# Layer 1 attention in a two-layer kernel: each of a pair's two heads in its own 64 contraction rows

## The reference

```python
xn = _layernorm(x, axis=-1)
x = x + _L1_attn_ref(xn, Wq, Wkv, Wo, bo) + _L1_ffn_ref(xn, inter_w, inter_b, output_w, output_b)
# in _L1_attn_ref: H = 32 heads, G = 8 groups, HD = 16, REP = 4
scores = jnp.einsum('bhqd,bhkd->bhqk', q, k)
scores = jnp.where(causal, -jnp.inf, scores)
weights = jax.nn.softmax(scores * (1.0 / HD ** 0.5), axis=-1)
ctx = jnp.einsum('bhqk,bhkd->bhqd', weights, v)
return jnp.dot(ctx, Wo) + bo
```

## Time and profile before

| | us |
|---|---|
| median of 3 runs | 1771.76 |
| lowest and highest run | 1762.22, 1773.39 |
| span of the profiled execution | 1769.7 |
| granted TensorE clock, mean over the span | 0.980 |

### The profile page before, as it was taken

How to read it: one execution, slowest core, us unless ns; L and a number is a source line. 1 busy time by engine, 2 the same in 40 slices (tenths; PEclk the granted TensorE clock), 3 DMA queues, 4 the chain that set the end, 5 groups by cost and what they waited for, 6 DMA issues and landing times. The chain is left out here.

```text
span 1769.7 us, 27326 instructions
## 1 busy us (share of the span) xinstructions
PE 1668.8 (94%) x8874; PEld 1226.8 (69%) x8874; DVE 1089.3 (62%) x2491; ACT 849.2 (48%) x1595; POOL 708.5 (40%) x735
## 2 busy tenths in 40 slices
PE   6899998999989999999999999789999999999998
PEld 5688887888766666666666666477765555568887
DVE  3556658999747777776777776335657677510222
ACT  3456556443326555555555555344135565653321
POOL 1112213444647566665566665386001111222221
PEclk9999999999999999999999999899979999999999
DMA  7522323220200001000001000364532343131111
GB/s 244 167 73 85 95 84 83 59 66 22 77 13 1 19 19 37 19 19 19 19 19 37 19 19 13 98 203 140 159 48 50 64 81 64 45 98 62 48 48 48
DMA packets 110717, 114.16 MB, mean 65 GB/s; under 512 B 39521, under 2 KB 71745, under 8 KB 110593
## 3 DMA queue, kind: packets, MB, share of 16 engines
q1 hardware_dynamic: 108288, 108.40, 21.8%
q10 hardware_dynamic: 2304, 4.20, 0.6%
HBM read 83.97 MB, written 28.44 MB: 64 GB/s over the span
## 5 line engine op out<-in xcount | busy, mean ns | idle before, releaser
L1490 POOL TENSOR_SCALAR a_p<-a_p,a_rinv 128x640 f32<-128x640 f32 (+7 forms) x256 | 190.6, 748 | 172.6 <-DVE a_rinv L1416 171.6
L1447 ACT ACTIVATE a_p<-a_sm,a_nmax 128x640 f32<-128x640 f32 (+7 forms) x256 | 198.6, 777 | 111.6 <-DVE a_nmax L1408 109.1
L1408 DVE CUSTOM_DVE_ANT_0 a_sm<-ps,maskb 128x640 f32<-128x640 f32 (+7 forms) x256 | 192.5, 752 | 94.7 <-PE ps L1352 91.2
L2334 DVE CUSTOM_DVE_ANT_0 ga_sm<-ps,strip 128x640 f32<-128x640 f32 (+1 forms) x224 | 163.2, 754 | 78.8 <-PE ps L2241 77.3
L2354 ACT ACTIVATE ga_pt<-ps 128x1024 f32<-128x1024 f32 (+1 forms) x192 | 148.1, 810 | 114.8 <-PE ps L2264 114.1
L1364 PE MATMUL ps<-ident,a_p 128*128 128x128 f32 x1152 | 172.1, 274 | 10.6 <-DVE a_pt L1423 10.4
L1364 PEld LDWEIGHTS ps<-ident,a_p 128*128 128x128 f32 x1152 | 132.9, 140 | 33.6 <-issue 10.5
L2394 POOL TENSOR_SCALAR_AFFINE_SELECT ga_pt<-ga_pt 128x512 f32<-128x512 f32 x64 | 40.6, 634 | 286.5 <-ACT ga_pt L2354 286.5
L1379 PE MATMUL ps<-a_pt,vst 128*64 128x512 f32 (+3 forms) x768 | 152.4, 506 | 1.8 <-DVE a_pt L1423 1.1
L1459 ACT COPY a_pt<-ps 128x512 f32<-128x512 f32 x128 | 74.2, 580 | 151.8 <-PE ps L1364 100.0
L1352 PE MATMUL ps<-kh,lq_qh 128*128 128x512 f32 (+3 forms) x384 | 131.7, 397 | 15.4 <-DVE a_nmax L1408 10.6
(11 more groups left out here) (319 smaller groups left out, 3972.1 us busy)
## 6 DMA issues: line engine op xcount, KB each, us to landing
ctx_d<-a_ctxst SPq DMA_DIRECT2D x16, 512.0 KB, 2.9
idx<-ctx_d SPq DMA_DIRECT2D x32, 256.0 KB, 3.8
idx<-wvo_d SPq DMA_DIRECT2D x32, 256.0 KB, 4.5
ga_qst<-qkd SPq DMA_DIRECT2D x42, 128.0 KB, 4.2
f_wr<-in_L_ffn_w SPq DMA_DIRECT2D x18, 256.0 KB, 2.7
x<-in_L_attn_hidden_states SPq DMA_DIRECT2D x16, 256.0 KB, 3.9
op_wo<-in_L_attn_o_w SPq DMA_DIRECT2D x8, 512.0 KB, 4.5
ix_w<-in_L_attn_idx_wq_w SPq DMA_DIRECT2D x64, 64.0 KB, 1.9
```

What stands on the lines that cost most here:

```text
L1408: dve.tensor_tensor_reduce(out=sm[kind][:, 0:w], in0=slots[kind][:, 0:w], in1=maskb[:, MASK_OFF[t]:MASK_OFF[t + 1]], scale=-scale, scalar= ...
L1447: act.activation(p[kind][:, v // 2 % 2, 0:w], sm[kind][:, 0:w], ACT.Exp, bias=nmax[:, v % 4:v % 4 + 1], scale=-1.0, accum_out=rsum[:, v % ...
L1490: pool.tensor_scalar(mine, mine, rinv[:, v % 4:v % 4 + 1], 1.0, ALU.mult, ALU.mult).then_inc(norm_done, 1)
L2334: dve.tensor_tensor_reduce(out=sm[kind][:, 0:w], in0=slots[kind][:, 0:w], in1=strip[:, S - w:], scale=-1.0, scalar=3.0e38, op0=ALU.add, op ...
```

## The change

The two heads of a pair are put 64 rows apart: a = 0 in rows 0 to 47 and a = 1 in rows 64 to 111 (`TILE1` = 64). The keys stand in both places of a single `kst`, without a copy for each a and without zeros. Each score product reads only its head's own rows, 48 of them for `score` and 49 for `keys`, where row 48 (or 112) of `qst` is the head's shift and that of `kst` is 1. Number, width, order, waits and PSUM targets of the matmuls stay, and so do number and size of the transfers. `kst` is prepared by one POOL memset over the whole tile to 1.0, after step 7, in place of POOL's three and DVE's two, and SP waits for that one.

```diff
--- before.py
+++ after.py
@@ -112,7 +112,7 @@
 ATTENTION0 += names("lq_", "raw_in tab_in wh_done wl_done q_mm q_evac add_done qh_done q_lo_done")
 ATTENTION0 += names("oq_", "", raw_in_=4)
 TO_QUERIES = names("oq_", "x_done stat var_done std_done rstd_done xn_done turned xh_done xl_done wh_done wl_done done "
-                   "hi_done lo_done ones_done zero_a zero_b", split_done_=4, cl_done_=4, wvl_done_=4, used_=4, stored=5,
+                   "hi_done lo_done ones_done", split_done_=4, cl_done_=4, wvl_done_=4, used_=4, stored=5,
                    w_in=2)
 LAYER1 = names("", "inv_done norm_done inv_out", raw_out=2, sum_in=2, ctx_in=2, scale_in=2)
 LAYER1 += names("ah_", "high low hidden b1_in", **{"in": 2})
@@ -1690,7 +1690,7 @@
 
 NB1 = 3
 KR1 = 3 * HD1
-KQ1 = 2 * KR1
+TILE1 = 64
 UNITS1 = REP1 * ST
 
 
@@ -1704,7 +1704,7 @@
     b = g % NB1
     sp.wait_ge(first["nt_done"], START + g + 1)
     for h in range(REP1):
-        r0 = KQ1 + h % 2
+        r0 = TILE1 * (h % 2) + KR1
         sp.dma_start(f32(qst[r0:r0 + 1, b, h // 2]).rearrange("o (t n) -> o t n", n=P),
                      nT[h * ST:(h + 1) * ST, g % 2]).then_inc(first["shift_in"][b], 16)
 
@@ -1716,10 +1716,10 @@
     k_v = qkd[:, D:, :].rearrange("l (g p) t -> g l p t", p=HD1)
     for a in range(2):
         for r, l in enumerate((0, 0, 1)):
-            r0 = KR1 * a + r * HD1
-            sp.dma_start(f32(kst[r0:r0 + HD1, b, a, at]), k_v[g][l][:, at]).then_inc(k_in[b], 16)
+            r0 = TILE1 * a + r * HD1
+            sp.dma_start(f32(kst[r0:r0 + HD1, b, at]), k_v[g][l][:, at]).then_inc(k_in[b], 16)
         for r, l in enumerate((0, 1, 0)):
-            r0 = KR1 * a + r * HD1
+            r0 = TILE1 * a + r * HD1
             sp.dma_start(f32(qst[r0:r0 + HD1, b, :, at]), q_v[g][a][l][:, :, at]).then_inc(q_in[b], 16)
 
 
@@ -1783,9 +1783,9 @@
         cr, wr = four(ctxn, 0), four(ctxn, 2)
         slots = [ps[:, 4 + 2 * k:6 + 2 * k, :].rearrange("p b n -> p (b n)") for k in range(2)]
         names = ("x_done", "stat", "var_done", "std_done", "rstd_done", "xn_done", "turned", "xh_done", "xl_done",
-                 "wh_done", "wl_done", "done", "hi_done", "lo_done", "ones_done", "zero_a", "zero_b")
+                 "wh_done", "wl_done", "done", "hi_done", "lo_done", "ones_done")
         (x_done, stat, var_done, std_done, rstd_done, xn_done, turned, xh_done, xl_done, wh_done, wl_done, done,
-         hi_done, lo_done, ones_done, zero_a, zero_b) = (c.sem("oq_" + n) for n in names)
+         hi_done, lo_done, ones_done) = (c.sem("oq_" + n) for n in names)
         split_done, cl_done, wvl_done, used = (
             c.sems(f"oq_{n}_", NS) for n in ("split_done", "cl_done", "wvl_done", "used"))
         stored, w_in = c.sems("oq_stored", NT1), c.sems("oq_w_in", 2)
@@ -1822,8 +1822,7 @@
                         sp.dma_start(qkd[l][m * P:(m + 1) * P, at], f32(o[:, m, at])).then_inc(stored[m], 16)
                     if m == 0:
                         if h == 0:
-                            sp.wait_ge(zero_a, START + 2)
-                            sp.wait_ge(zero_b, START + 3)
+                            sp.wait_ge(ones_done, START + 2)
                         sp.wait_ge(stored[NQ], START + 32 * (h + 1))
                         sp.wait_ge(stored[0], START + 32 * (h + 1))
                         load_group(sp, qkd, qst, kst, q_in, k_in, 0, at)
@@ -1847,12 +1846,7 @@
                     if (half, k) == (0, 5):
                         pool.memset(v32[:, :, :, HD1:], 1.0).then_inc(ones_done, 1)
                     if (half, k) == (0, 7):
-                        pool.memset(f32(kst[:, :, 1]), 0.0).then_inc(zero_b, 1)
-                        pool.wait_ge(zero_b, START + 1)
-                        pool.memset(f32(kst[KQ1:KQ1 + 2, :, 1]), 1.0).then_inc(zero_b, 1)
-                        pool.wait_ge(zero_b, START + 2)
-                        pool.memset(f32(kst[KQ1:KQ1 + 1, :, 1]), 0.0).then_inc(zero_b, 1)
-                        pool.wait_ge(zero_b, START + 3)
+                        pool.memset(f32(kst[:, :, :]), 1.0).then_inc(ones_done, 1)
 
             @block.scalar
             def _(act):
@@ -1956,11 +1950,6 @@
                 for half, k, s, u in steps:
                     dve.wait_ge(split_done[s], START + u + 1)
                     dve.tensor_tensor(cl[:, s], cr[:, s], f32(ch[:, s]), ALU.subtract).then_inc(cl_done[s], 1)
-                    if (half, k) == (0, 6):
-                        dve.memset(f32(kst[:, :, 0]), 0.0).then_inc(zero_a, 1)
-                    if (half, k) == (0, 8):
-                        dve.wait_ge(zero_a, START + 1)
-                        dve.memset(f32(kst[KQ1:KQ1 + 1, :, 0]), 1.0).then_inc(zero_a, 1)
                     if half == 0:
                         continue
                     if k in (2, 3):
@@ -2015,10 +2004,11 @@
                     if v >= 2:
                         pe.wait_ge(first["max_done"], START + v - 1)
                     wide = (t + 1) * P
+                    mine = slice(TILE1 * (h % 2), TILE1 * (h % 2) + KR1)
                     for k0 in range(0, wide, HALF):
                         k1 = min(k0 + HALF, wide)
-                        ins = pe.matmul(slots[v % 2][:, k0:k1], qst[0:KQ1, 0, h // 2, t * P:(t + 1) * P],
-                                        kst[0:KQ1, 0, h % 2, k0:k1], start=True, stop=True)
+                        ins = pe.matmul(slots[v % 2][:, k0:k1], qst[mine, 0, h // 2, t * P:(t + 1) * P],
+                                        kst[mine, 0, k0:k1], start=True, stop=True)
                     ins.then_inc(first["scored"], 1)
 
                 def task(n):
@@ -2149,7 +2139,6 @@
     LAG = 2
     LEAD = 3
     SCALE = HD1 ** -0.5
-    KQ = KQ1
     STEPS = [(0, j) for j in range(4)] + [(1, j) for j in range(8)]
     NSTEP = len(STEPS)
     UNITS = UNITS1
@@ -2236,10 +2225,11 @@
                     if n >= 2:
                         pe.wait_ge(max_done, START + n - 1)
                     w = (t + 1) * P
+                    mine = slice(TILE1 * (h % 2), TILE1 * (h % 2) + KR1)
                     for k0 in range(0, w, HALF):
                         k1 = min(k0 + HALF, w)
-                        ins = pe.matmul(slots[kind][:, k0:k1], qst[0:KQ, b, h // 2, t * P:(t + 1) * P],
-                                        kst[0:KQ, b, h % 2, k0:k1], start=True, stop=True)
+                        ins = pe.matmul(slots[kind][:, k0:k1], qst[mine, b, h // 2, t * P:(t + 1) * P],
+                                        kst[mine, b, k0:k1], start=True, stop=True)
                     ins.then_inc(scored, 1)
 
                 def turn(g):
@@ -2261,8 +2251,9 @@
                     if s == NSTEP - LEAD + 1 and g + 1 < G1 and p == 0:
                         pe.wait_ge(nt_done, START + g + 2)
                     for a in range(2):
-                        ins = pe.matmul(ps[:, 2 * p + a, 0:q1 - q0], kst[0:KQ + 2, b, a, j * P:(j + 1) * P],
-                                        qst[0:KQ + 2, b, p, q0:q1], start=True, stop=True)
+                        mine = slice(TILE1 * a, TILE1 * a + KR1 + 1)
+                        ins = pe.matmul(ps[:, 2 * p + a, 0:q1 - q0], kst[mine, b, j * P:(j + 1) * P],
+                                        qst[mine, b, p, q0:q1], start=True, stop=True)
                     ins.then_inc(st_done[p], 1)
 
                 def weigh(g, s):
@@ -2724,7 +2715,7 @@
                 ci = Ctx(nc, inner)
                 v32 = ci.sb("v32", [P, ST, G1, 2 * HD1])
                 qst = ci.sb("ga_qst", [P, NB1, 2, S], F32R)
-                kst = ci.sb("ga_kst", [P, NB1, 2, S], F32R)
+                kst = ci.sb("ga_kst", [P, NB1, S], F32R)
                 nmax = ci.sb("ga_nmax", [P, 2, UNITS1])
                 nT = idx[0:UNITS1, DT * S:DT * S + 2 * P].rearrange("p (k n) -> p k n", k=2)
                 q_in, k_in = ca.sems("ga_q_in", NB1), ca.sems("ga_k_in", NB1)
```

## The result

| | before | after |
|---|---|---|
| median of four runs, us | 1772.6 | 1838.4 |
| lowest and highest, us | 1762.2, 1773.9 | 1837.6, 1842.4 |
| span of the profiled execution, us | 1769.7 | 1835.9 |
| granted clock, mean over the span | 0.980 | 0.910 |

The ratio is 1.038 (95% interval 1.034 to 1.042): 66 us slower. The forecast was 1802 with a range of 1740 to 1830. Its direction and its cause hold, its size doesn't: twice the loss that was worked out.

What follows compares the result with a forecast made beforehand. PE was taken to have the most work but to be held in a loop with DVE and ACT. Span 1769.7 - 7.5 (memsets) + 3 (projections) + 5 (first group) + 33 (groups 1 to 6) - 1 (last) = 1802 us, range 1740 to 1830.

Steps and rivals of the forecast that it cites:

- The memsets: In outputs_to_queries, one POOL memset for three removes PE's hole and the low clock behind it: -7.5 us (0 to -8).
- Row halves side by side: In attention, a pair's two keys products overlap, up to 4.5 us a group off PE; score gains under 1.
- the prediction's own sign: In the profile after: keys starts of a pair 0.23 us apart, not some ns, would make the overlap step wrong.
- What the overlap is worth: In attention groups 1 to 6, a full-clock group goes from 33.5 to 31 us (bounds 29 and 33.5).
- I count a bit over half: Share of the PE overlap saving in attention expected to come through the loop with DVE: 33.5 to 31 us a group.
- A group at the low clock: An attention group run wholly at clock 0.50 takes 43 us.
- How much of the pace is low: Groups 1 to 6 run two thirds of their pace at 0.50: 39 us each, +33 us over six.
- The projections: Before attention, 24 places where 48-row products stand among 128-row ones cost shape changes: +3 us (0 to twice that).
- First and last group: Attention's first group, mostly low already, +5 us; last group regains the clock, -3 with +2 for shape changes, so -1.
- The clock holds: Rival: only busy time counts, so attention stays at clock 1.00 and gains from overlap: 1746 us, chance 0.23.
- Low clock and no overlap: Rival: attention loses the clock and halves don't overlap, six groups +69 us: about 1845 us, chance 0.07.
- always low: Upper bound of the clock term for groups 1 to 6, at 0.50 throughout: +57 us.

Runs made afterwards that it cites:

- spread_memsets: Kernel before, with POOL's three memsets at steps 7, 12 and 19 of outputs_to_queries instead of all after step 7: 1764.8 us, ratio 0.9971.
- rows64_short: rows64 with DVE's maximum over only the first 256 keys of a row: 1743.1 us, ratio 0.986 to the kernel before.
- rows64: Changed kernel with zero query rows added, so products run over 63 (score) and 64 (keys) rows: 1798.6 us, ratio 1.016 to the kernel before.
- all128: Changed kernel's 64-row spacing, but a zero-padded key copy per head and both products over all 128 rows: 1759.6 us, ratio 0.9950 to the kernel before.
- pairs_serial: Changed kernel with both heads of a pair in the same half and the two pairs in opposite halves: 1863.2 us, ratio 1.052 to the kernel before.
- filler1: Changed kernel plus one overwritten 128-row, 512-wide matmul before each step's first keys product: 1906.9 us, ratio 1.075 to the kernel before.
- keys64_scores128: all128 with only the keys products cut to their head's 64 rows: 1780.3 us, ratio 1.006 to the kernel before.
- scores64_keys128: all128 with only the score products cut to their head's 64 rows: 1890.4 us, ratio 1.068 to the kernel before.

## Why the prediction was wrong in size and right in cause

**The memsets: right.** -7.5 predicted, and -7.5 measured from the matmuls ahead of the gap to those behind the low stretch, in after and in spread_memsets alike.

**Row halves side by side: right that they do, wrong in which.** The step had the two `keys` products of a pair run together and gave `score` under 1 us, because a product that needs the same half stands between most units. With 10 of 144 pairs starting together in groups 1 to 6, it is `keys` and score products that overlap. By the prediction's own sign (pair starts 0.23 us apart) the step as worded fails. That the total comes near, 4.8 us a group in rows64_short, which runs mostly at full clock, against 4.5 and under 1, is luck.

**What the overlap is worth: too high.** The prediction took 31 us for a group at the full clock. A full-clock group of after doesn't exist. In rows64 the groups of 20.5, 17 and 10.2 us of low time take 37.8, 37.0 and 35.4 us, 0.23 us for each low microsecond, which leads to 33.0 with none; with the sixth group too (3.4 us low, 32.5 us long) it is 0.30 and 31.8. I take 0.27 and 32.6 (an estimate). The failing step is "I count a bit over half": of 4.5 us only about 0.8 came through against all128's 33.4 (0.4 to 1.6 by the two ways), because DVE's loop takes the rest. At the low clock the prediction had 7.7 between a group with and without overlap. No run shows that: pairs_serial takes away 2.6 of 9.1 us of overlap and is 4.1 us a group longer.

**A group at the low clock: nearly right.** 43 predicted; 44.4 measured with 41 us of it low, so about 45 with all of it low, by the 0.27 above (an estimate).

**How much of the pace is low: the main miss.** The prediction put two thirds of a group's pace at 0.50, which no row gave: it was chosen between never and always. Of the time, 84% was low; with 45 and 32.6 us that is 0.80 of the pace (0.80 x 45 + 0.20 x 32.6 = 42.5, measured 42.6). With the prediction's own prices 0.80 makes 40.6 us a group, 1.6 over its 39, so 10 of the 22 us that were missed in six groups come from the share, and the other 12 from the two prices, 2 and 1.6 us too low.

**The projections: the other miss, and a plain one.** The step priced only the change of shape there, +3, and the stage grew by 16.0. The changes of shape come to what was priced: at the full clock the first score of the eighth place starts 9.0 us after that of the first and not 8.0, 0.13 a place, so 24 take +3. But a round costs some 0.4 us and not 0.16 (an estimate from the starts around one place: 0.32 us into the score products where 0.23 is usual, 0.39 for two of 384 columns side by side where one took 0.18 before, 0.34 behind them where 0.23), and the two score products that now run together give half of it or more back. So the sum is right by luck. Timeline of after at 1.00 (answers to the earlier trace rows; the two score products are 48 rows):

```profile
1259.90 0.46 PE L2010 MATMUL ps<-ga_kst,ga_qst 48*128 48x384 f32 x2
1260.28 0.50 PE L155 MATMUL ps<-xnh,ah_l 128*128 128x512 f32 x1
1260.62 0.39 PE L156 MATMUL ps<-xnl,ah_l 128*128 128x512 f32 x1
1260.85 0.40 PE L157 MATMUL ps<-xnh,oq_wl 128*128 128x512 f32 x1
```

The `mm3` matmul after a score has 0.34 us to the next, and the second of a row 0.23. The rest is the clock: from 1271.2 to its first score of attention after needs 35.4 us, for matmuls that take before 20.7. Windows of some 24 us in this stage, of before and then of after:

```profile
1271.00:1295.00 24.00, 21.55 (x130) 18.08 (x129) 19.29 (x44) 2.75 (x9) 0.00 (x0) 1.00 0.60 136
```

```profile
1271.20:1295.00 23.80, 23.80 (x70) 16.30 (x69) 12.48 (x25) 1.07 (x4) 0.00 (x0) 0.50 0.38 58
```

Before, 130 matmuls in 24 us, PE busy for 90% and the clock at 1.00. After, 70 matmuls in 23.8 us, PE busy throughout and the clock at 0.50, from 1271.2 and not from 1295.6. The prediction reasoned about rows for the six groups and forgot the 24 places where the same 48-row products stand between 128-row ones.

**First and last group: right.** +6 and -1.6 for +5 and -1. In the last group, with its dense 128-row matmuls, the clock is 1.00 throughout (from 1602), as said.

**The rivals.** *The clock holds* fell with PEclk 0.58. *Low clock and no overlap*, at 1845, is near the measured time by chance: after overlaps for 9.1 us a group. With the measured +55 in place of +33 the sum is 1824, still inside the range, as its bound of "always low" (+57) allowed; what took the time out of it are the 13 us that the projections grew over their +3. That term's bounds, 0 and twice +3, had nothing for the clock.

## What to carry to other kernels

Before a product is cut to a part of the array's rows, look at the granted clock of the stretch, and of the stages before it that hold the same products: one on half the rows that runs alone does half the work for each microsecond, and what it saves in zeros it can lose in clock. Zeros up to 128 rows cost PE nothing here. Whether they gain time over 96 rows isn't shown. And look in the trace which products really run together: here it was not the pair that the change was made for. And an overlap on PE is worth only what the loop that feeds it lets through: take the wait for the other engine away in one run to see how much that is.

## What the runs showed of the hardware

- The granted clock goes with the rows in use, zeros counted in: in the same schedule 48/49 rows give 0.58 over groups 1 to 6, 63/64 give 0.79, 96/98 give 1.00, with a drop in the profile of spread_memsets, 126/128 and 128/128 give 1.00. PE's busy share doesn't order them: 92, 87, 92, 92 and 92%; filler1 has 99.4% and 0.51. The Trainium skill's account ("TensorE: Matmul & The Clock Gate", Part 1) goes by how busy the engine is, and doesn't fit filler1's row.
- Two products on opposite row halves start 0 to 10 ns apart where nothing else holds a half (all 192 pairs of keys64_scores128). In after, where score products hold the halves too, each half goes at its own pace, and in 74 of 192 pairs the product issued second starts first, by up to 0.9 us.
- Going from 128-row to 64- or 48-row products and back costs some 0.4 us a round at the full clock, in the projections and in scores64_keys128. The Trainium skill names the drain ("TensorEngine Tiling (Array Packing)", Key Properties) without a price.
- A 128x512 product at 0.50 has 0.72 us to the next start when products on 48-row halves follow (filler1). Two 98-row ones together take 0.85 us, 0.43 each.
